# Cross-attention phase of a transformer block: value products copied into one of two output buffers and multiplied by the inverse sums in place

## The reference, cut to what matters

```python
xn = layer_norm(x, ln1_w, ln1_b)
q = _heads(xn @ q_w.T)
k = _heads(codebook_embeds @ k_w.T)
v = _heads(codebook_embeds @ v_w.T)
attn = jnp.einsum('bhnd,bhmd->bhnm', q, k) * SCALE
bias = (1.0 - codebook_mask.astype(attn.dtype))[:, None, None, :] * -10000.0
attn = jax.nn.softmax(attn + bias, axis=-1)
ca = _merge(jnp.einsum('bhnm,bhmd->bhnd', attn, v)) @ ca_proj_w.T
x = x + ca
```

## Time and profile before

| | |
|---|---|
| time before, median of 3 runs | 3685.34 us |
| the profiled execution's own time | 3683.99 us |
| its span | 3682.2 us |
| granted TensorE clock, mean | 0.94 |
| PE busy | 3365.0 us (91%) |
| DVE busy | 2215.5 us (60%) |
| ACT busy | 1545.2 us (42%) |
| POOL busy | 1701.3 us (46%) |

### The profile page before, as it was taken

The page is one execution under the profiler, slowest core; times in us unless marked ns, Lnnn a source line. Parts: engine busy times, 40 slices in busy tenths (PEclk is TensorE's granted clock), DMA queues, the critical chain, the costliest instruction groups (busy, mean ns, idle before and its releaser), DMA issues. The chain is left out here.

```text
span 3682.2 us, 52183 instructions
## 1 busy us (share of the span) xinstructions
PE 3365.0 (91%) x16432; PEld 2104.9 (57%) x16432; DVE 2215.5 (60%) x3731; ACT 1545.2 (42%) x2794; POOL 1701.3 (46%) x507
## 2 busy tenths in 40 slices
PE   7998999999999999999999668898876689999999
PEld 6885544444444444444444156556535568888887
DVE  4445878887888888888888125666644632222222
ACT  3230666666666666666666512442422321111111
POOL 0001788888888888888878622342322200000000
PEclk9997999999999999999999887898957889999999
DMA  4547347465465746546553453333315741111110
GB/s 171 180 163 183 71 100 161 87 133 116 96 131 107 155 86 140 115 97 131 107 118 74 106 146 95 116 112 108 90 53 206 263 163 46 46 46 46 46 46 23
DMA packets 178499, 412.01 MB, mean 112 GB/s; under 512 B 20289, under 2 KB 43399, under 8 KB 158831
## 3 DMA queue, kind: packets, MB, share of 16 engines
q1 hardware_dynamic: 156271, 273.87, 24.4%
q0 software_dynamic: 18432, 134.23, 18.2%
q10 hardware_dynamic: 3584, 1.05, 0.1%
HBM read 146.08 MB, written 102.56 MB: 68 GB/s over the span
## 5 line engine op out<-in xcount | busy, mean ns | idle before, releaser
L1591 DVE TENSOR_REDUCE self_part_max<-self_first 128x1 f32<-128x512 f32 x2048 | 1277.9, 676 | 299.9 <-PE self_first L1448 296.6
L1549 ACT ACTIVATE self_expo<-self_second 128x512 f32<-128x512 f32 x2048 | 1068.0, 603 | 690.0 <-PE self_second L1464 656.4
L1397 POOL TENSOR_TENSOR self_pair_sum<-self_expo 128x2048 f32<-128x2048 f32 x192 | 882.8, 4598 | 117.4 <-ACT self_expo L1549 93.9
L1448 PE MATMUL self_first<-self_k,self_q 96*128 96x512 f32 x2048 | 884.6, 439 | 40.9 <-DVE self_part_max L1591 24.2
L1464 PE MATMUL self_second<-self_q,self_k 98*128 98x512 f32 x2048 | 813.4, 400 | 13.5 <-ACT self_expo L1549 13.4
L1448 PEld LDWEIGHTS self_first<-self_k,self_q 96*128 96x128 f32 x2048 | 394.6, 193 | 559.1 <-DVE self_part_max L1591 445.2
L1477 PE MATMUL self_weighted<-self_expo,self_v_sb 128*32 128x512 f32 x4096 | 546.3, 605 | 9.1 <-ACT self_unscaled L1561 6.9
L1464 PEld LDWEIGHTS self_second<-self_q,self_k 98*128 98x128 f32 x2048 | 388.5, 190 | 109.6 <-ACT self_expo L1549 47.7
L1943 DVE CAST mlp_h_high<-mlp_h 128x512 fp32r<-128x512 f32 x128 | 54.7, 427 | 505.6 <-PE mlp_out_sum L61 504.6
L1918 ACT ACTIVATE mlp_h<-mlp_hidden_sum,mlp_b_col 128x512 f32<-128x512 f32 x128 | 88.0, 688 | 601.1 <-PE mlp_hidden_sum L61 601.1
L1397 POOL TENSOR_TENSOR self_half_sum<-self_expo 128x2048 f32<-128x2048 f32 x64 | 292.7, 4579 | 82.9 <-ACT self_expo L1549 82.9
(11 more groups left out here) (165 smaller groups left out, 4130.7 us busy)
## 6 DMA issues: line engine op xcount, KB each, us to landing
self_half_sum<-self_pair_sum POOLq DMA_DIRECT2D x128, 1024.0 KB, 7.2
self_k<-k_t SPq DMA_DIRECT2D x96, 256.0 KB, 9.7
self_q<-q_t SPq DMA_DIRECT2D x93, 256.0 KB, 4.5
cross_q<-cross_r_high SPq DMA_DIRECT2D x256, 64.0 KB, 2.0
qkv_x<-in_x SPq DMA_DIRECT2D x8, 1024.0 KB, 5.4
v<-qkv_v_sb SPq DMA_DIRECT2D x32, 256.0 KB, 2.0
q_t<-qkv_r_high SPq DMA_DIRECT2D x32, 256.0 KB, 2.0
q_t<-qkv_r_low SPq DMA_DIRECT2D x32, 256.0 KB, 2.3
```

The costliest lines, as they stand in the source:

```text
L1397: nc.gpsimd.tensor_tensor(to, expo[:, t % p_slots], expo[:, (t + 1) % p_slots], ALU.add).then_inc(pair_done, 1)
L1448: nc.tensor.matmul(first[:, in_ring[n]], q[0:base, c % q_slots, a, s * P:(s + 1) * P], k[0:base, c // stages_per_group % 2, a, k0:k0 + TOK ...
L1549: nc.scalar.activation(expo[:, t % p_slots, a], second[:, n % ring], ACT.Exp, scale=scale).then_inc(exp_done, 1)
L1591: nc.vector.tensor_reduce(part_max[:, a * SUB + s, k:k + 1], first[:, in_ring[n]], AX_X, ALU.max).then_inc(first_read, 1)
```

## The change

The buffer `unscaled` is gone. The copy writes straight into `mean[:, n % 2]`, and the multiply works on that buffer in place. The copy no longer waits for `mean_done`; it waits for the store of the same buffer two groups earlier (`out_stored`), a wait that stood on the multiply and is taken off it. n % 2 and g % 2 are the same, since a tile has 4 groups. Nothing else is edited, and no instruction is moved, added or left out.

```diff
@@ -575,7 +575,6 @@
-        unscaled = m.sbuf("unscaled", [P, TOK])
         mean = m.sbuf("mean", [P, 2, TOK])
@@ -974,8 +973,8 @@
                 def take_weighted(t, g):
                     n = groups * t + g
                     act.wait_ge(weighted_done, n_k * (n + 1))
-                    ge(act, mean_done, n)
-                    nc.scalar.activation(unscaled[:], weighted, ACT.Copy).then_inc(weighted_read, 1)
+                    ge(act, out_stored[n % 2], 16 * (n // 2))
+                    nc.scalar.activation(mean[:, n % 2], weighted, ACT.Copy).then_inc(weighted_read, 1)
@@ -1102,8 +1101,7 @@
                     dve.wait_ge(weighted_read, n + 1)
-                    ge(dve, out_stored[g % 2], 16 * (n // 2))
-                    nc.vector.tensor_tensor(mean[:, g % 2], total[:], unscaled[:], ALU.mult).then_inc(mean_done, 1)
+                    nc.vector.tensor_tensor(mean[:, g % 2], total[:], mean[:, g % 2], ALU.mult).then_inc(mean_done, 1)
```

## The result

The changed kernel takes 3722.89 us, the median of 4 runs (3718.74 to 3733.31); the kernel before, beside it, 3686.41 us (4 runs, 3683.68 to 3693.85). The ratio is 1.0098, with a 95% interval of 1.008 to 1.0116: **slower by 36 us**. The prediction said 3723. The profiled execution took 3733.31 us, at the upper end of the four; 7.8 of the 49 us between it and the profiled execution of before had gone by when the first copy started (2261.26 against 2253.46), in work that the change doesn't touch. So the two traces are compared inside the cross phase.

What follows compares the result with a forecast made beforehand. TensorE, busy nearly all the time, was taken as the bound. Terms 33.0 + 10.9 + 0.7 - 6.2 = +38.4 us on the profiled 3683.99 gave 3722.4; with 1.35 to the median 3723.7, stated as 3723, range 3702 to 3760.

Steps and rivals of the forecast that it cites:

- The copy loses its wait: ScalarE's copy 0 in a steady tile can start when exponential 5 is done, 1.36 us earlier, its new wait costing nothing.
- rival A: The store comes in time, the new wait never ends last, and 25.6 us go: 3659.7 us; chance 0.05.
- The ring: Copy, stack of DMAs, store, copy through SyncE's queue: 13.35 us from copy to copy, where the old ring took 9.07.
- TensorE: In steady tiles 1 to 5 the value product of group 3 starts 6.6 us late: +33.0 us in all.
- the 3.7 to spare: TensorE's 3.7 us left before copy 2 absorb a slower stretch, so the hole at copy 1 counts as free.
- Tile 6: No projection covers copy 3, which comes at 2696.2 against 2685.31: +10.9 us.
- Tile 0: Copy 2 slips about 2 us, but TensorE is late anyway: +0.7 us, between -2 and +6.6.
- Tile 7: Without stacks, stores land in time and 2.05 us of wait fall away before three copies: -6.2 us.
- The multiply in place: Reading and writing one buffer, the multiply takes 0.69 us as before: 0 counted.
- Rival B: TensorE's clock falls too: 3739 us with slow first passes (3 us a tile), 3808 if projections also slow; chance 0.18.
- a clock well below that of before in a steady tile: One of three signs that the forecast is wrong, concerning TensorE's granted clock; no size given.
- the threshold: Copy 1 would be free of waiting for the store if a stack's issuing took under 2.8 us; loss ends at 4.7.

## Why the prediction was right, point by point

1. *The copy loses its wait.* Right: copy 0 of a steady tile waits for nothing. The bound of 25.6 us for what hangs on the old wait (rival A) was too low: two copy buffers gained 34 us, 0.92%. I took TensorE's own work of a group as 8.1 us, the 9.07 between copies less the hole of 1.00 that the profile shows; without the ring it was 7.6, so the hole had cost 1.5 a group. The other part of the miss is the clock in tile 0 (point 5).
2. *The ring.* Right in mechanism and nearly in size. Copy to stack 2.95 us expected, 2.94 to 2.95 found; stack 8.0, found 7.52 to 8.04 in tile 2; landing and start 2.4, found 2.36. The 18 gaps of tiles 1 to 6 average 13.0 us (12.8 to 13.9), against 13.35.
3. *TensorE.* The tile comes out 6.6 us longer, as tiles 2 and 3 do (72.2 - 65.2 = 7.0; 71.7 - 65.2 = 6.5), but by two errors that cancel. The ring was 0.15 to 0.5 us a gap shorter. And the hole before copy 1, which I counted as free, was not: TensorE's 10.5 us of work behind it took 14.6 (2416.04 to 2430.64), at a granted clock of 0.52 over most of it. Those 4.1 us are more than the 3.7 to spare, of which the shorter ring had also taken 0.5: the value product of group 3 began 0.9 us later than its inputs allowed, 2.9 us after copy 2 and not 2.0. And only two tiles of five are such tiles: against before, tiles 1 and 5 are 10.5 and 10.6 us longer, so the five together are 40.9 longer and not 33.0.
4. *Tile 6* +10.9 expected, +9.8 found. As counted here the tile ends with copy 0 of tile 7, whose 2.05 us I had put under tile 7; so 8.85 is the number to compare, and the tile lost 1 us more than that.
5. *Tile 0* +0.7 expected, -7.6 found. Its low-clock stretches shrank from 30.7 to 10.2 us. All kernels here that dropped the old wait and whose profile was read show 10.2 to 13.7 us there; of the three with the old wait two show 30.7 and one 13.7. So this is a gain that can come with the change, and that I hadn't in the sum.
6. *Tile 7* -6.2 expected. Its copies moved together by 2.15 us each, of which two lie behind copy 0 (-4.4 found) and one ahead of it, in what is counted as tile 6. The sum's term is right to 0.3 us.
7. *The multiply in place* at no cost: 0.69 us as before, and shown by the kernel with the store first.

Rival B, that the clock falls too, was in part true and stood beside the forecast, not against it. Tiles 1, 4 and 5 spent 34 to 38 us at the lower clock and lasted 75.8 to 77.1 us, 4 to 5 more than tiles 2 and 3. Before, tiles 0 and 4 had done the same. I had named a clock well below that of before in a steady tile as a sign of being wrong, and in tiles 1, 4 and 5 it came. Tile 1 before, then tiles 1 and 2 after (us, PE busy, PEld, DVE, ACT, POOL busy, granted clock, DMA share, GB/s):

```profile
2325.69:2391.04 65.35, 57.42 (x307) 36.88 (x306) 42.46 (x66) 25.43 (x45) 23.87 (x6) 0.92 0.38 114
2325.84:2401.71 75.87, 66.20 (x307) 43.55 (x306) 42.95 (x67) 25.36 (x47) 23.82 (x6) 0.78 0.33 100
2401.71:2473.89 72.18, 61.20 (x307) 38.30 (x306) 42.46 (x67) 25.35 (x47) 23.83 (x6) 0.86 0.35 103
```

The first hole was not free, then, and the 3.7 us did not absorb what followed; a first pass at the lower clock, put at 3 us a tile, came with 4 to 5 in three tiles. What kept the total right is that before had lost nearly as much to its clock in tiles 0 and 4. Tile 0's -7.6 and the extra of tiles 1, 4 and 5 are why the sum of +38.4 met a measured +38.7 from the first copy to the last multiply. That match is of two single executions, the one after 10 us above its median; by the medians the change costs 36.5 us, and the kernel before was 3686.41 and not 3685.34. (The sum gives 3723.7, which rounds to 3724.) The hit to within a microsecond is luck, the sign and the mechanism are not. Rival A, that the store comes in time, is what happens when the store is issued ahead of the DMAs, and nearly so behind four of them: I had put the threshold at 2.8 us of issuing ahead of the store; with TensorE's 7.6 us in place of 8.1 it is 2.3, four DMAs are 2.5, and their copies stand mostly 8.1 us apart. The loss itself, by my reckoning, begins at 4.7 us; the runs put it between 2.5 and 5.0.

The Trainium skill (DMA: Bandwidth & Descriptors, section "Issuing engines are not separate DMA queues") says that the sequencer's time to initiate a DMA is usually small relative to the DMA itself. For one DMA the trace doesn't contradict it: twelve issues in 7.52 us are 0.63 each, against 2.0 from issue to landing. My "the trace disagrees" set twelve issues against one landing. What the rule doesn't count is the sum: the store stands behind 7.5 us of issuing, and with the store ahead of it the loss is gone.

## What to carry to other kernels

A wait that moves to an earlier instruction must be priced anew, at the moment when the awaited thing really comes: a store wait that cost nothing on the multiply cost more on the copy than the wait it replaced, because the store is issued by an in-order queue behind twelve DMAs that themselves wait for an instruction behind the copy before it. Before reusing a buffer that a DMA reads, write down the ring (who frees it, what is queued ahead of its issue, who releases that) and compare its length with the bound engine's work for one step. Here a ring just above that work (8.1 against 7.6 us) cost 0.14%, within the noise, one of 10.3 us and more cost 1.3%, and the change's of 13.0 cost 2.0%, each against the store first. Moving the store ahead of the stack turned +1.0% into -1.1%.

## What was not expected of the hardware

One hole of 5.16 us in TensorE's work was followed by some 9 us at the lower level of its clock, with the engine busy all the time, and 10.5 us of work took 14.6. With idle products in the hole the same work took 10.4 us (2411.40 to 2421.83). So the spare time behind such a hole should not be counted in full. Smaller holes do it too, but not each time: with 1.0 us of hole a group, tiles 2 and 3 before spent 10.2 us at the lower level and tile 4 30.7; why the one and not the other, no run here shows.
